# A routed-expert kernel: h of tiles 7 to 18 turned by DMA transposes of its words, and several small moves around it

## The chip, the cores and the metric

The kernel runs on one core of a Trainium2 chip. The core has TensorE (PE) with its weight loads (PEld), VectorE (DVE), ScalarE (ACT), GpSimd (POOL), SyncE (SP) and 16 DMA engines, each with its own list of instructions; semaphores order the lists against each other. The metric is the device time of one execution in microseconds, of which less is better.

## The reference

There are B=4 sequences of S=512 tokens with D=512 features. A layernormed x goes through a gated block whose weights are the context rows themselves; of four contexts each token takes the one that its id chooses. Then comes a mixture of six feed-forward experts, of which each sequence takes its top two:

```python
def _L0_xattn_ref(hidden_states, token_ids, Wg, Wu, Wd):      # Wg = Wu = Wd = ctx (4, 512, 512)
    expert_ids = jnp.minimum(tid // tokens_per_expert, E - 1)
    for e in range(E):
        g = jax.nn.silu(jnp.einsum('bsd,fd->bsf', hidden_states, Wg[e]))
        u = jnp.einsum('bsd,fd->bsf', hidden_states, Wu[e])
        y = jnp.einsum('bsf,df->bsd', g * u, Wd[e])
        out = jnp.where((expert_ids == e)[..., None], y, out)
...
    gate_probs = jax.nn.softmax(jnp.einsum('bd,ed->be', x.mean(axis=1), gate_W))
    topk_vals, topk_idx = jax.lax.top_k(gate_probs, TOP_K)    # renormalised to sum 1
    h = gelu(jnp.einsum('bsd,bkdf->bksf', x, W1[topk_idx]) + b1)      # F2 = 352
    eo = jnp.einsum('bksf,bkfd->bksd', h, W2[topk_idx]) + b2
    return jnp.einsum('bk,bksd->bsd', topk_vals, eo)
...
x = x + jnp.tanh(g_xattn[0]) * xattn(layernorm(x), ids, ctx)
x = x + jnp.tanh(g_ffn[0]) * ffn(layernorm(x))
```

Each product is made of split operands, a high part and a low part (hi·hi + lo·hi + hi·lo).

## The kernel before

**Stages.** After a setup that sorts the tokens by expert come TILES = 19 tiles of 128 sorted rows, one expert each (tile stage, some 30 to 145 us), and then four batches b = 0 to 3 of the second block.

**A tile.** GpSimd gathers the rows of tile j into one of RING places of x_ring (L502) and later writes the result back by a scatter (L511). VectorE takes the rows' mean and variance (rows_statistics, L661), GpSimd makes the inverse root (inverse_root, L506), VectorE normalises into h (L683). TensorE turns h by four transposes into bank 0 (transpose_h, L1192, its matmul at L1196); ScalarE copies the high part hT_hi (h_high, L965), VectorE makes the low part hT_lo (h_low, L689). The first product (12 matmuls, L1214) goes to bank 3, ScalarE takes silu of it (silu_of, L975), VectorE multiplies (up, L702) into a; TensorE turns a (transpose_a, L1199, L1205), a_high (L970) and a_low (L696) split it, and the second product (12 matmuls) gives y, which VectorE adds to x_ring (add, L668), with statistics for the second block (L673).

**The order of a step.** TensorE's step j is: turn a(j-1), turn h(j+1), first product of j, second product of j-1 (tile_step, L1313, and from PREP = 12 on the loop at L1422). ScalarE's is a_high(j-1), silu_of(j), h_high(j+1) (L1020). VectorE's is a_low, add, rows_statistics(j+2), statistics, up(j), normalise(j+2), h_low(j+1) (L754). GpSimd's is, tile by tile, inverse root, scatter, wait for an older scatter, gather (L555). All orders are written out by hand. In steps 12 to 18 work of batch 0 is put between: its rows are normalised and turned, ffn_h_high (L1024) splits them, the logits (L1349) and the gate (scale_logits, exponents, choose) follow.

**A batch.** hidden products with the first of two weight sets, gelu (L1065), output products, then the same with the second set. Weights come by SP's queue (load_experts, L403) and are split by ScalarE (split_high, L1056) and VectorE (split_low, L816). In batches 1 and 2 the normalised rows of the batch after are turned on the side: ScalarE parts the 32-bit words into their 16-bit halves (part_words, L1034), SP issues a DMA transpose of them (L454), and ScalarE joins the halves (join_words, L1043). ScalarE's list starts such a batch like this (L1105):

```python
if joined_ahead:
    split_high(b, 1, 2)
gelu_of(b, 0, 0, chosen)
```

where split_high(b, 1, 2) waits for w2 and the b2 rows of the second set, copies the b2 rows (L1062) and rounds w2 (L1063).

## Time and profile before

| | us |
|---|---|
| median of 3 runs (lowest, highest) | 281.7 (279.95, 281.95) |
| profiled execution | 281.29 |
| its span on the core | 279.5 |
| TensorE busy in the span | 272.1 (97%) |
| VectorE | 216.2 (77%) |
| ScalarE | 133.5 (48%) |
| GpSimd | 70.2 (25%) |

An engine's busy time counts its instructions alone, not its waits. Matmuls are pipelined: one that takes 0.39 us may start 0.23 after the one before. In rows of a timeline the first number is the start in us, the second the length, then engine, line, operation, what it writes and reads, and in brackets the idle time before it with what ended it. The chain of waits follows the last instruction back through what released it.

### The profile page before, as it was taken

The numbers are of one execution on the slowest core, as the hardware profiler recorded it, in microseconds if no ns is written. First come the engines' busy times: TensorE is split into PE (matmuls) and PEld (weight loads), VectorE is DVE, ScalarE is ACT, GpSimd is POOL, SyncE is SP. The second block draws the span as 40 slices with busy tenths as digits, with TensorE's granted clock in tenths as the row PEclk, the third lists the DMA queues.
The fourth block names the chain that finished last, engine by engine and source line by source line (L and its number), as shares of the span: only waits on it lengthen the run. The fifth ranks groups of instructions, "written<-read, shape, count | busy, mean of one in ns | idle before, by whom it ended". The sixth has DMA issues, their size and how long they took to land.

```text
span 279.5 us, 4519 instructions
## 1 busy us (share of the span) xinstructions
PE 272.1 (97%) x1400; PEld 222.3 (80%) x1400; DVE 216.2 (77%) x500; ACT 133.5 (48%) x216; POOL 70.2 (25%) x113
## 2 busy tenths in 40 slices
PE   8999999999999999999999999979999999999995
PEld 7878888888888888888778867858778777888783
DVE  8889888867777889687996669869698775958073
ACT  4844322223222233373628183889677995534020
POOL 5565265645444555324133000000000000000000
PEclk9999999999999999999999999999999999999999
DMA  6870042223255222319702717994199603940004
GB/s 214 290 254 0 5 119 105 79 75 111 82 135 199 82 75 78 75 45 300 205 38 87 240 53 233 228 276 151 31 306 211 189 0 113 315 160 2 0 0 150
DMA packets 32610, 37.10 MB, mean 133 GB/s; under 512 B 12584, under 2 KB 21038, under 8 KB 32588
## 3 DMA queue, kind: packets, MB, share of 16 engines
q1 hardware_dynamic: 29376, 26.69, 33.4%
q0 software_dynamic: 3040, 9.98, 11.4%
q8 instruction: 12, 0.20, 0.3%
q10 hardware_dynamic: 172, 0.15, 0.2%
q14 instruction: 10, 0.08, 0.1%
HBM read 25.52 MB, written 9.19 MB: 124 GB/s over the span
## 4 chain that ended last, share of the span: by engine, by line
PE 77%; SPq 6%; DMA 6%; ACT 5%; DVE 2%; issue 2%; DVEq 0%; ACTq 0%
PE bank L1214 38%; PE bank L1188 9%; PE bank L1189 8%; PE bank L1190 8%; DMA b_rows<-in_L_ffn_b 4%; PE bank L1205 3%; PE bank L1196 3%; PE bank L1266 3%; DMA raw_ctx<-in_ctx 2%; ACT w_hi L1063 2%; SPq L438 1%; DVE x_even L880 1%; SPq L435 1%; ACT act L1070 1%; SPq L433 1%
## 5 line engine op out<-in xcount | busy, mean ns | idle before, releaser
L1188 PE MATMUL bank<-w_lo,ctx_hi 128*128 128x512 f32 x80 | 31.7, 397 | 0.6 <-DVE ctx_lo L872 0.6
L1190 PE MATMUL bank<-w_hi,ctx_lo 128*128 128x512 f32 x80 | 31.2, 390 | 0.0
L1189 PE MATMUL bank<-w_hi,ctx_hi 128*128 128x512 f32 x80 | 31.2, 390 | 0.0
L978 ACT ACTIVATE a<-bank 128x512 f32<-128x512 f32 x19 | 11.4, 598 | 40.5 <-PE bank L1214 40.5
L973 ACT ACTIVATE aT_hi<-bank 128x512 fp32r<-128x512 f32 x18 | 10.8, 598 | 33.9 <-PE bank L1205 31.8
L1063 ACT ACTIVATE w_hi<-w_raw 128x512 fp32r<-128x512 f32 (+3 forms) x24 | 23.8, 1018 | 3.9 <-DMA w_raw<-in_L_ffn_W 3.9
L1188 PE MATMUL bank<-ctx_lo,w_hi 128*128 128x512 f32 x60 | 23.8, 397 | 1.2 <-ACT act L1070 1.2
L1214 PE MATMUL bank<-ctx_hi,hT_hi 128*128 (+1 forms) x80 | 23.3, 413 | 0.3 <-ACT hT_hi L968 0.3
L1189 PE MATMUL bank<-ctx_hi,w_hi 128*128 128x512 f32 x60 | 23.4, 391 | 0.0
L1190 PE MATMUL bank<-ctx_hi,w_lo 128*128 128x512 f32 x60 | 23.4, 390 | 0.0
L503 POOL DMA_INDIRECT x_ring<-in_x,get_rows x19 | 19.3, 1017 | 14.1 <-DVE put_rows L653 9.2
L871 DVE TENSOR_SCALAR ctx_hi<-act,mix 128x512 fp32r<-128x512 f32 x16 | 7.8, 486 | 19.3 <-ACT act L1070 19.2
L1070 ACT ACTIVATE act<-bank,tables 128x512 f32<-128x512 f32 x16 | 10.9, 684 | 22.9 <-PE bank L1190 22.8
L1214 PE MATMUL bank<-ctx_hi,hT_lo 128*128 (+1 forms) x80 | 21.6, 392 | 0.0
L1214 PE MATMUL bank<-ctx_lo,hT_hi 128*128 (+1 forms) x80 | 21.5, 391 | 0.0
L515 POOL DMA_INDIRECT x_scratch<-x_ring,put_rows x19 | 20.1, 1056 | 5.4 <-POOL x_ring L514 5.4
L698 DVE TENSOR_TENSOR aT_lo<-bank,aT_hi 128x512 fp32r<-128x512 f32 x18 | 12.4, 687 | 10.3 <-ACT aT_hi L973 10.3
L508 POOL TENSOR_TENSOR rstd<-ve,half 128x1 f32<-128x1 f32 x19 | 10.8, 570 | 36.2 <-DVE ve L666 36.2
L1214 PE MATMUL bank<-ctx_hi,aT_hi 128*128 (+1 forms) x72 | 19.9, 398 | 0.0
L1214 PE MATMUL bank<-ctx_hi,aT_lo 128*128 (+1 forms) x72 | 19.6, 392 | 0.0
L1214 PE MATMUL bank<-ctx_lo,aT_hi 128*128 (+1 forms) x72 | 19.3, 390 | 0.0
L1188 PEld LDWEIGHTS bank<-w_lo,ctx_hi 128*128 128x128 f32 x80 | 15.0, 188 | 4.6 <-issue 1.4
(221 smaller groups left out, 625.7 us busy)
## 6 DMA issues: line engine op xcount, KB each, us to landing
raw_ctx<-in_ctx SPq DMA_DIRECT2D x4, 1024.0 KB, 6.7
w_raw<-in_L_ffn_W SPq DMA_DIRECT2D x8, 512.0 KB, 4.8
x_even<-x_scratch SPq DMA_DIRECT2D x8, 257.0 KB, 3.9
w_raw<-in_L_ffn_W SPq DMA_DIRECT2D x8, 256.0 KB, 2.9
w_raw<-in_L_ffn_W SPq DMA_DIRECT2D x4, 448.0 KB
out<-x_even SPq DMA_DIRECT2D x7, 256.0 KB, 2.4
w_raw<-in_L_ffn_W SPq DMA_DIRECT2D x4, 384.0 KB, 7.2
x_odd<-x_scratch SPq DMA_DIRECT2D x4, 257.0 KB, 3.6
```

Source lines behind the costliest of these rows:

```text
L503: pool.indirect_dma_start(x_ring[:, r * DS:r * DS + D], None, x_rows, bass.IndirectOffsetOnAxis(get_rows[:, j:j + 1], 0)).then_inc(gathere ...
L508: pool.tensor_tensor(rstd1[:, :], ve1[:, :], half[:, 0:1], ALU.pow).then_inc(rstd_ready, 1)
L515: pool.indirect_dma_start(x1_rows, bass.IndirectOffsetOnAxis(put_rows[:, j:j + 1], 0), x_ring[:, r * DS:(r + 1) * DS], None).then_inc(scat ...
L698: dve.tensor_tensor(lo[:, :, :].rearrange("p k t -> p (k t)"), bank[:, :], hi[:, :, :].rearrange("p k t -> p (k t)").bitcast(FP32), ALU.su ...
L973: sc.activation(aT_hi[:, :, :].rearrange("p k t -> p (k t)"), aT_ps[:, :], ACT.Copy).then_inc(aT_hi_done, 1)
L978: sc.activation(a[:, :], z_bank(j)[:, :], ACT.Silu).then_inc(silu_done, 1)
L1063: sc.activation(part_of(w_hi[s], piece, s), part_of(w_raw[s], piece, s), ACT.Copy).then_inc(hi_done[s], 1)
L1070: sc.activation(act[:, c % 2, :], hid_ps[k % 2][:, :], ACT.Gelu, bias=b1_of(s, c, slice(0, P), chosen[s])).then_inc(gelu_done, 1)
L1188: pe.matmul(dst, s_hi, m_lo, start=first, stop=False)
L1189: pe.matmul(dst, s_hi, m_hi, start=False, stop=False)
L1190: return pe.matmul(dst, s_lo, m_hi, start=False, stop=last)
L1214: return pe.matmul(dst[:, :], src[:, k, :], weights[:, bass.ds(e * (KD * F1) + k * F1, F1)], start=first, stop=last)
```

## The change

1. **h of tiles 7 to 18** (TURNED = 7) is no longer turned by TensorE. VectorE normalises three tiles ahead instead of two (row_step). ScalarE parts h's words into halves (part_row), SP issues a DMA transpose for each tile (seven ahead of load_x1(0) in its list, five behind it), ScalarE joins the halves into hT_joined and copies that to hT_hi (join_row), ahead of silu_of, and VectorE's h_low reads hT_joined instead of the bank.
2. **GpSimd in the tile stage:** the ring has eight places (the eighth, x_eighth, in a region of act), the inverse root is made one tile further ahead and stands first in the loop, and one extra root stands behind the scatter of tile 3.
3. **The gate's exponents** go from ScalarE (Exp, with table loads) to GpSimd (a power of e); the logits of batch 0 and choose(0) stand one step later, and ffn_h_high(0) is spread over two steps. The splits of the first weights of batch 0 stand behind the tile loop.
4. **Batches 1 and 2:** the b2 rows are loaded ahead of the second weights; ScalarE's list starts with gelu; GpSimd rounds 128x1536 of w2 (round_w2) and joins the first quarter of the turned words (join_first).

Core of the diff ("..." marks what is left out):

```diff
-    RING = 7
+    RING = 8
+    TURNED = E + 3
...
+        def turned(j):
+            return TURNED <= j < TILES
         def hT_of(j):
-            return (hT1_hi, hT1_lo) if j == 1 else (hT_hi, hT_lo)
+            return (hT1_hi, hT1_lo) if j == 1 or (turned(j) and j % 2) else (hT_hi, hT_lo)
...
+                for e, rows in ((one, (64, 65, 96)), (two, (66, 67, 97))):
+                    for row in rows:
+                        sp.dma_start(b2_rows[row:row + 1, :], b2[bass.ds(e, 1), :]).then_inc(w2_here[1], 16)
                 sp.dma_start(part_of(second, 0), w1_cols(two, MB, MB + P)).then_inc(w1_here[1], 16)
...
+            turn_row_words(range(TURNED, EARLY + TURNED))
             sp.wait_ge(tiles_landed, EARLY)
             load_x1(0)
+            turn_row_words(range(EARLY + TURNED, TILES))
             sp.wait_ge(rows_done, 1)
             sp.wait_ge(pads_made, 2)
             load_experts(0)
...
             for j in range(1, TILES):
                 paired = j + 2 in PAIRED or j + 3 in PAIRED
-                if paired and j + AHEAD < TILES:
-                    inverse_root(j + AHEAD)
+                ahead_of = j + AHEAD + (j > TURNED - AHEAD)
+                if j == PREP + 2:
+                    exponents(0)
+                if paired and ahead_of < TILES:
+                    inverse_root(ahead_of)
                 scatter(j, j % RING)
...
+                if j == TURNED - AHEAD:
+                    inverse_root(ahead_of + 1)
                 landed(j - 1)
...
+            for b in range(0, B - 1):
+                if by_dma(b + 1):
+                    round_w2(b)
+                    join_first(b + 1)
+                exponents(b + 1)
...
+            def row_step(j, between=None):
+                add(j - 2, y_ps)
+                a_low(j - 1)
...
+                if j + 3 < TILES:
+                    rows_statistics(j + 3)
+                statistics(j - 2)
+                if j + 3 < TILES:
+                    normalise(j + 3)
+                up(j)
+                if j + 1 < TILES:
+                    h_low(j + 1)
...
+                    if j == TURNED - 2:
+                        rows_statistics(j + 3)
+                        normalise(j + 3)
...
+            def tile_step(j, between=None):
+                a_high(j - 1)
+                if turned(j + 1):
+                    join_row(j + 1)
+                if between:
+                    between()
+                silu_of(j)
+                if j + 1 < TURNED:
+                    h_high(j + 1)
+                if j == TURNED - 2:
+                    part_row(TURNED)
+                if j >= TURNED - 2 and turned(j + 3):
+                    part_row(j + 3)
...
-                if joined_ahead:
-                    split_high(b, 1, 2)
                 gelu_of(b, 0, 0, chosen)
                 split_high(b, 1, 0)
                 split_high(b, 1, 1)
                 gelu_of(b, 0, 1, chosen)
+                split_high(b, 1, 2)
                 if joined_ahead:
-                    join_words(b + 1, [0, 1])
-                else:
-                    split_high(b, 1, 2)
+                    join_words(b + 1, [1])
                 gelu_of(b, 0, 2, chosen)
...
                 transpose_a(j - 1)
-                if j in PAIRED:
+                if j in PAIRED and not turned(j + 1):
                     transpose_h(j + 1)
...
-                if j == PREP + 3:
+                if j == PREP + 4:
                     logits(0)
                 transpose_a(j - 1)
-                if j == PREP + 3:
-                    pe.wait_ge(neg_max_ready, 1)
-                if j + 1 < TILES:
-                    transpose_h(j + 1)
                 first_product(j, e)
```

How the rows of an engine's list move is shown at three places. In these rows a name's number tells one buffer from another, x2 means two alike, and brackets name the semaphores waited for.

TensorE's list at the start of step 6, before:

```order
L1209 ISA x2
L1205 MATMUL bank1<-ident,a 128x128 [waits aT_lo_done,a_ready]
L1205 MATMUL bank1<-ident,a 128x128 x3
L1196 MATMUL bank0<-ident,h 128x128 [waits hT_lo_done,h_ready]
L1196 MATMUL bank0<-ident,h 128x128 x3
L1214 ISA [waits a_ready,hT_hi_done]
L1214 MATMUL bank3<-ctx_hi_49,hT_hi 128x512
```

And of the changed kernel at the same place:

```order
L1307 ISA x2
L1303 MATMUL bank1<-ident,a 128x128 [waits aT_lo_done,a_ready]
L1303 MATMUL bank1<-ident,a 128x128 x3
L1312 ISA [waits a_ready,hT_hi_done]
L1312 MATMUL bank3<-ctx_hi_49,hT_hi 128x512
```

The four turns of h are gone, and the first product follows the turn of a.

ScalarE's list of steps 5 to 7, before (a<-bank3 is silu, hT_hi<-bank0 is h_high, aT_hi<-bank1 is a_high):

```order
L978 ACTIVATE a<-bank3 128x512 [waits z_done]
L968 ACTIVATE hT_hi<-bank0 128x512 [waits z_done,hT_done]
L973 ACTIVATE aT_hi<-bank1 128x512 [waits y_done,aT_done]
L978 ACTIVATE a<-bank3 128x512 [waits z_done]
L968 ACTIVATE hT_hi<-bank0 128x512 [waits z_done,hT_done]
```

And of the changed kernel:

```order
L1057 ACTIVATE a<-bank3 128x512 [waits z_done]
L1047 ACTIVATE hT_hi<-bank0 128x512 [waits z_done,hT_done]
L1103 ACTIVATE row_words_59<-h 128x1024 [waits h_ready] x2
L1052 ACTIVATE aT_hi<-bank1 128x512 [waits y_done,aT_done]
L1111 ACTIVATE hT_joined1_62<-row_words_T_60 128x2x512 [waits z_done,row_words_turned1]
L1113 ACTIVATE hT1_hi_57<-hT_joined1_62 128x512 [waits row_words_joined]
L1057 ACTIVATE a<-bank3 128x512 [waits z_done]
L1103 ACTIVATE row_words_59<-h 128x1024 [waits row_words_turned1,h_ready]
L1052 ACTIVATE aT_hi<-bank1 128x512 [waits y_done,aT_done]
```

Two partings (tiles 7 and 8) stand ahead of a_high(5), and the joining and copying of tile 7 ahead of silu of tile 6.

ScalarE's list at the start of batch 1, before (w_lo1<-b2_rows copies the b2 rows, act<-bank is gelu):

```order
L1062 ACTIVATE w_lo1<-b2_rows 64x512 [waits o_done,w2_here1]
L1063 ACTIVATE w_hi1<-w_raw1 128x1536
L1070 ISA [waits hid_done,a2_ready]
L1070 ACTIVATE act_53<-bank3,tables 128x512
L1063 ACTIVATE w_hi1<-w_raw1 128x512 [waits o_done,w1_here1]
```

And of the changed kernel:

```order
L1176 ISA [waits hid_done,a2_ready]
L1176 ACTIVATE act_53<-bank3,tables 128x512
L1169 ACTIVATE w_hi1<-w_raw1 128x512 [waits o_done,w1_here1]
L1169 ACTIVATE w_hi1<-w_raw1 128x4x192 [waits o_done,w1_rest_here1]
L1176 ISA [waits hid_done,a2_ready]
L1176 ACTIVATE act_53<-bank2,tables 128x512
L1165 ACTIVATE w_lo1<-b2_rows 64x512 [waits o_done,w2_here1]
```

The wait for w2_here1 stands behind two gelus now, and the rounding of 128x1536 has left the list.

## Rows read from the trace of the kernel before

**Rows 1.** The page's first part: busy us, share of the span, instructions.

```profile
PE 272.1 (97%) x1400; PEld 222.3 (80%) x1400; DVE 216.2 (77%) x500; ACT 133.5 (48%) x216; POOL 70.2 (25%) x113
```

**Rows 2.** Chain of waits in order of time, 99 to 130: start, us, what.

```profile
100.38 0.44 PE bank L1205 x4
100.82 0.44 PE bank L1196 x4
...
115.15 0.59 PE bank L1205 x4
...
128.50 0.63 PE bank L1196 x4
```

**Rows 3.** Busy us (instructions) by stretch, granted clock, DMA share, GB/s; step 6.

```profile
core 0: us, PE busy (x) PEld busy (x) DVE busy (x) ACT busy (x) POOL busy (x), PEclk, DMA share, GB/s
55.79:62.12 6.33, 6.33 (x33) 5.33 (x32) 4.88 (x11) 1.68 (x3) 3.04 (x5) 1.00 0.28 83
```

**Rows 4.** Instructions of words and words_T: duration ns min/median/max, first and last start.

```profile
L1040 ACT ACTIVATE words<-h x8: 1037/1041/1043, 175.6 to 212.3; 128x1024 uint16<-128x1024 uint16 x8
...
L454 SPq DMA_TRANSPOSE words_T<-words x8: 1292/1330/3289, 176.9 to 215.4; - x8
L1048 ACT ACTIVATE joined<-words_T x8: 1341/1355/1380, 186.9 to 224.6; 128x1024 uint16<-128x1024 uint16 x8
...
DMA to landing us min/median/max: 3.2/4.2/5.8
```

**Rows 5.** Timeline of VectorE, 82 to 89: the start of a tile's statistics and of the next.

```profile
83.72 0.68 DVE L664 BATCH_NORM_STATS2 stats<-x_ring 128x6 f32<-128x512 f32 x1
...
84.72 0.68 DVE L675 BATCH_NORM_STATS2 stats<-x_ring 128x6 f32<-128x512 f32 x1
```

**Rows 6.** Timeline of all engines, 54 to 60, around the start of step 6.

```profile
54.50 0.54 DVE L686 TENSOR_SCALAR h<-x_ring,mv,rstd 128x512 f32<-128x512 f32 x1
...
54.83 1.13 POOL L515 DMA_INDIRECT x_scratch<-x_ring,put_rows  x1 [0.29 <-POOL x_ring L514]
...
54.95 0.69 DVE L692 TENSOR_TENSOR hT_lo<-bank,hT_hi 128x512 fp32r<-128x512 f32 x1
...
56.42 0.60 ACT L973 ACTIVATE aT_hi<-bank 128x512 fp32r<-128x512 f32 x1 [2.08 <-PE bank L1205]
...
59.39 0.84 PE L1214 MATMUL bank<-ctx_hi,aT_hi 128*128 x3
...
59.59 0.60 ACT L978 ACTIVATE a<-bank 128x512 f32<-128x512 f32 x1 [2.58 <-PE bank L1214]
```

**Rows 7.** Timeline of TensorE, 182 to 189 and 220 to 222.

```profile
183.65 0.39 PE L1190 MATMUL bank<-ctx_hi,w_lo 128*128 128x512 f32 x1
185.25 0.50 PE L1188 MATMUL bank<-ctx_lo,w_hi 128*128 128x512 f32 x1 [1.20 <-ACT act L1070]
...
188.59 0.47 PE L1188 MATMUL bank<-w_lo,ctx_hi 128*128 128x512 f32 x1 [0.29 <-DVE ctx_lo L872]
...
221.25 0.47 PE L1188 MATMUL bank<-w_lo,ctx_hi 128*128 128x512 f32 x1 [0.32 <-DVE ctx_lo L872]
```

**Rows 8.** Timeline of all engines, 174 to 186.

```profile
174.79 2.03 SPq L438 DMA_DIRECT2D b_rows<-in_L_ffn_b  x6
...
182.49 0.63 ACT L1062 ACTIVATE w_lo<-b_rows 64x512 fp32r<-64x512 f32 x1 [1.56 <-DMA b_rows<-in_L_ffn_b]
...
184.53 0.67 ACT L1070 ACTIVATE act<-bank,tables 128x512 f32<-128x512 f32 x1
...
185.23 0.49 DVE L871 TENSOR_SCALAR ctx_hi<-act,mix 128x512 fp32r<-128x512 f32 x1 [1.97 <-ACT act L1070]
```

**Rows 9.** GpSimd's groups by shape: count | busy us, mean ns | idle before, releaser.

```profile
L508 POOL TENSOR_TENSOR rstd<-ve,half 128x1 f32<-128x1 f32 x19 | 10.8, 570 | 36.2 <-DVE ve L666 36.2
...
L500 POOL TENSOR_SCALAR w_raw<-col_h,pslot 128x128 f16<-128x128 f16 x3 | 2.0, 674 | 2.5 <-DVE pslot L631 2.5
...
L489 POOL MEMSET b_rows<- 128x512 f32 x1 | 0.5, 514 | 0.0
```

**Rows 10.** One line's instructions (L640, sorting): duration ns min/median/max, first and last start.

```profile
L640 DVE TENSOR_SCALAR w_raw<-col_h,pslot x13: 241/248/345, 6.1 to 8.1; 128x128 f16<-128x128 f16 x13
```

More of the change, by code:

```diff
@@ L221, in flamingo_kernel, with ring_place @@
         a2_lo = ctx_lo[:, 2 * KD * S:(2 * KD + FC) * S].rearrange("p (c t) -> p c t", t=S)
-        x_ring = sb("x_ring", [P, RING * DS])
+        x_ring = sb("x_ring", [P, (RING - 1) * DS])
+        x_eighth = at("x_eighth", [P, DS], FP32, place[1])
+        def ring_place(r, start, size):
+            return x_eighth[:, start:start + size] if r == RING - 1 else x_ring[:, r * DS + start:r * DS + start + size]
         used = [IDC * 2 * TILES // 2]
@@ L658, in ring_row @@
             def ring_row(j, start, size):
[L659 removed]
+                return ring_place(j % RING, start, size)
             def rows_statistics(j):
@@ L816, in split_low @@
             def split_low(b, s, piece):
-                place = (1, 2, 0)[piece] if s == 1 and by_dma(b + 1) else piece
-                dve.wait_ge(hi_done[s], len(PARTS) * b + place + 1)
+                dve.wait_ge(hi_done[s], len(PARTS) * b + piece + 1)
+                if s == 1 and piece == 2 and by_dma(b + 1):
+                    dve.wait_ge(w2_rounded, b)
                 raw, hi, lo = w_raw[s], w_hi[s], w_lo[s]
@@ L883, in _ @@
             for j in range(PREP, TILES):
-                if j == PREP + 3:
-                    scale_logits(0)
-                add(j - 2, y_ps)
-                a_low(j - 1)
-                if j + 2 < TILES:
-                    rows_statistics(j + 2)
-                statistics(j - 2)
-                up(j)
-                if j + 2 < TILES:
-                    normalise(j + 2)
-                if j + 1 < TILES:
-                    h_low(j + 1)
+                row_step(j, (lambda: scale_logits(0)) if j == PREP + 4 else None)
                 if j < PREP + 2:
```

137 lines of the change are left out of this document (89 added, 48 removed).

## The prediction

> **What bounds it now.** I read the page's first part, then the chain of waits in order of time, then the timeline stage by stage. TensorE is busy 272.1 of 279.5 us [rows 1], at a granted clock of 1.00 in the step whose window I show [rows 3] and in every other that I read. So a gain is work taken off PE, or a gap in PE's work that closes. In the chain a tile step is four turns of a(j-1), four turns of h(j+1), and the 24 matmuls of two products: the two groups of turns take 0.44 each, at 100.38 and 100.82 [rows 2]. In step 6 (55.79 to 62.12) VectorE works 4.88 of 6.33 us, ScalarE 1.68, GpSimd 3.04 [rows 3]. At two places a group of turns took longer, 0.59 at 115.15 and 0.63 at 128.50 [rows 2]: small waits, 0.34 in all. The other stretch to read is the turn from batch to batch, where PE does stand still [rows 7].
>
> **Term 1, the turns of h leave PE.** Tiles 7 to 18 are twelve, each with one group of four turns in a step: 12 x 0.435 = -5.2 us, and a step goes from about 6.35 to 5.92. This holds only if the new path (normalise, part into half words, DMA transpose, join, copy, low part) is ready for each step. The trace has its pieces already, since the batch stage turns its words in the same way: parting 1.04, the transpose 3.2/4.2/5.8 us from issue to landing, joining 1.36 [rows 4]; the copy to hT_hi is as large as that of aT_hi, 0.60 [rows 6].
>
> Steady state. VectorE keeps its eleven operations of a step, 4.88 us of 5.92 [rows 3]. ScalarE has 0.60 (a_high) + 1.36 + 0.60 (join, copy) + 0.60 (silu) + 1.04 (parting) = 4.2 of 5.92. From step 6, which begins at 55.79, a_high starts 0.63 later and silu 3.80 later [rows 6]; without the turn of h that is 3.4. In VectorE's new list add, a_low and two statistics stand ahead of normalise(j+3), which ends near S+4.3 (S: the step's start), and up(j) ends near S+5.0. Parting of tile j+3 runs from S+4.45 to S+5.5. Its joining stands behind a_high two steps later, at S + 11.84 + 1.23 = S+13.1. So a transpose may take 13.1 - 5.5 = 7.5 us with its handing over, and the longest of eight took 5.8 [rows 4]. PE sets the step, and this costs nothing: 1.7 us of cover over the longest, 3.3 over the median. If that cover is gone, up(j+1) is late by what goes beyond 7.5, at 0.5 to 1 us a step for each us of it, in eleven steps.
>
> **Term 2, the entry.** There the path isn't a step ahead yet, so I follow it through steps 5 to 7. h_low(6) ends at 55.64 [rows 6]. VectorE then takes the statistics of tile 8, 1.0 us from their first operation to the next one's start [rows 5]: 56.6. GpSimd's extra root stands behind the scatter that ends at 55.96 [rows 6], and takes 0.57 from 56.6 on [rows 9]: 57.2. normalise(8) takes 0.54 [rows 6]: 57.8. ScalarE parts it from 57.85 to 58.9, and only then comes a_high(5), which stands behind both partings now and started at 56.42 before [rows 6]: it ends at 59.4. PE reaches the second product of step 6, which began at 59.39 [rows 6], 0.435 earlier, at 58.96, and waits 0.45 for aT_hi.
>
> The words of tile 7 are parted behind its normalise (54.50 + 0.54, [rows 6]) from 55.1 to 56.2; their transpose lands at 59.4, 60.4 or 62.0 (3.2, 4.2, 5.8). Joining and copying (2.0) end at 62.4 by the median, silu(6) behind them at 63.0, up(6) (0.7) at 63.7. PE wants a(6) at 62.12 - 0.44 + 0.45 = 62.2: it waits 1.45. Bounds: 0.95 with the shortest landing (VectorE's list, which has normalise(9) ahead of up(6), holds it then), 3.0 with the longest. I take the median: 0.45 + 1.45 = **+1.9**, bounds +1.4 and +3.5. From step 8 on the lists are a step ahead.
>
> **Term 3, the rest of the tile stage.** The logits of batch 0 stand a step later and wait for the fourth piece of ffn_h_high, which is spread over two steps: +0.2, a third of one ScalarE copy of 0.6. The two small waits of the chain fall with the turns that had them: -0.34. Together **-0.1**. The exponents go from ScalarE to GpSimd's pow (as a root, 0.57, [rows 9]), and ScalarE's table loads go; in the chain neither holds PE: nothing.
>
> **Term 4, the batch turns.** At 183.65 PE starts a matmul, and the next only at 185.25, after a wait for gelu; the pitch is 0.23, so 1.37 is lost. ScalarE's list tells why: at 182.49 it copied rows of b2 after 1.56 us of waiting for their DMA, then rounded w2, and did the gelu at 184.53 [rows 8]. Two waits more, 0.29 at 188.59 and 0.32 at 221.25, are for low parts behind the same late copy [rows 7]; in the proportion of the first (1.37 lost for 1.20 shown) they cost 0.7 together. After the change gelu stands first, the rows of b2 are loaded ahead of the second weights, and GpSimd does the rounding: **-2.1**; from below nothing, if another wait takes the place (rival 1). What it moves: the six b2 issues take 2.03 us on SP's queue [rows 8], so the second weights go out that much later; ScalarE reads them behind its first gelu, and they have landed by then.
>
> GpSimd's price for this size the trace doesn't show. From below, a 128x512 memset in 0.51 is 1.0 ns an element, 1.5 us for 1536; from above, 128x128 in 0.67 is 5.3 ns, 8.1 us [rows 9]. The two joining copies of 512 are 0.5 to 2.7 each. I take 3 and 1 each, nearer the memset, which is nearer in size. From the b2 and w2 landing near 182.4 that ends at 187.5, or at 196 by the upper ends; the logits, which hang on the joined words, are wanted near 195 (the turn's PE work from 183.9 on). So the middle costs nothing, the upper end about 1 us in each of two turns.
>
> One page speaks against it. By the Trainium skill, "SBUF — State Buffer", section "SBUF: two separate sides", VectorE and GpSimd share a port pair as an exclusive lock for a whole instruction, so a VectorE operation with two SBUF inputs would stand until a GpSimd rounding that reads SBUF has ended. In this trace 13 VectorE operations took 0.241 to 0.345 us [rows 10] beside GpSimd's three of 0.67 [rows 9], and none was longer by one of these whole; no run here shows the lock with a wide GpSimd operation. What it would make of the time is rival 1.
>
> **Sum.** -5.2 + 1.9 - 0.1 - 2.1 = -5.5 from the profiled execution's 281.29 us (span 279.5 and 1.8 around it): 275.8. That execution is 0.4 below the median of the runs, 281.7, so against the median it is -2.1%.
>
> **Rivals.**
> 1. GpSimd takes ScalarE's place at the turns. At the middle of its two bounds the rounding is 4.8 us, 182.4 to 187.2. The next weighing on VectorE stood at 185.23 [rows 8] and is due at 184.6 when gelu follows PE; waiting for GpSimd's whole operation it loses 2.6, in two turns 5.2: 275.8 + 5.2 = **281.0**. For it: the two work side by side on wide tiles for the first time, and VectorE's low part of w2 waits for the rounding too. Against: [rows 10]. Half of it gives 278.4. Chance 0.12.
> 2. The lists make a step longer than PE does: up(j) stands behind normalise(j+3) in VectorE's list, and that behind a root and a parting. At 0.3 us in each of eleven steps it is 275.8 + 3.3 = **279.1**. For it: roots waited 36.2 us in all for VectorE's statistics [rows 9], so each is made in the last moment, and now stands between two operations of the same list. Against: 1.0 us of each step is free on VectorE, and a root is 0.57. Chance 0.13.
> 3. The other side: transposes land late, as SP's queue has loads of x1 between them and an issue took up to 3.3 us [rows 4]. From 7.5 us of latency steps lengthen; at 9.0 in every step it is 1.5 x 0.5 x 11 = +8.3, **284.1**, and from about 9.1 slower by over 1%. Against: the longest of eight was 5.8. Chance 0.07.
> 4. No change: the entry costs its upper bound (+1.6 more), the turns give nothing back (+2.1), and the steps are 0.2 longer (+2.2): **281.7**. Chance 0.06.
>
> **Numbers.** The forecast has 0.62, with a range of its own from 274 (entry at its lower bound, turns a little better) to 277.5 (entry at its upper bound). Within 1% of 281.7, about what a measurement of this kernel can tell from no change, is 278.9 to 284.5. Faster: the forecast, the milder half of 1 and of 2: 0.73. Slower: rival 3 and a trace of 1: 0.08. The rest: 0.19. The range 273.8 to 280.0 takes in rival 2 and half of 1, and leaves out 3, 4 and the full 1.
>
> **What would show it.** Right: no turn of h on PE after tile 6 and steps of 5.92; waits of PE of about 0.45 and 1.45 in steps 6 and 7 and nowhere else in the stage; joining waits for a DMA at tile 7 alone; the gap of 185.25 gone, since gelu no longer stands behind a DMA. Wrong: steps over 6.1, and what up waits for (root, parting or a landing) tells rival 2 from 3; a VectorE operation of several us beside GpSimd's rounding, or ScalarE and PE waiting for GpSimd's joining copies, is rival 1.

## The result, and the profile after

The changed kernel takes 277.67 us (median of 4, 277.57 to 278.45), the kernel before on the same occasion 281.61: a ratio of 0.987 with a 95% interval of 0.984 to 0.990, so 1.3% faster. On a second occasion it was 278.15 beside 281.57 (0.986, 0.983 to 0.990). The forecast was 275.8: right in its direction, in its range and in most of its places, and 1.9 us too good.

The page's first part of the changed kernel, to be read beside [rows 1]:

```profile
PE 267.1 (97%) x1352; PEld 217.6 (79%) x1352; DVE 220.6 (80%) x508; ACT 145.0 (52%) x213; POOL 91.5 (33%) x124
```

TensorE has 48 instructions less (twelve tiles of four turns) and 5.0 us less to do; ScalarE has 11.5 more and GpSimd 21.3 more. The span fell by 2.9 (279.5 to 276.6; the traced execution took 278.45).

Where the time went is seen by the same marks of TensorE's work in both traces:

| stretch of TensorE's work | before | after | difference | prediction |
|---|---|---|---|---|
| start to step 2 | 30.01 | 30.48 | +0.47 | 0 |
| step 2 to the turn of a(18) (from 140.67; from 137.93) | 110.66 | 107.45 | -3.21 | -3.4 |
| from there to the last matmul (275.77; 272.97) | 135.10 | 135.04 | -0.06 | -2.1 |

The first row is the first load of context, 5.30 us in one chain of waits and 5.77 in the other. In ten other traces, with an edit or without, it was 5.3 to 6.5; it differs from execution to execution. The tile stage came out as worked. Nearly the whole miss is in the batches.

**The tile stage.** Busy us by stretch (as [rows 3]) of step 6, the entry, and step 10 of the changed kernel:

```profile
core 0: us, PE busy (x) PEld busy (x) DVE busy (x) ACT busy (x) POOL busy (x), PEclk, DMA share, GB/s
56.44:64.08 7.64, 6.38 (x30) 4.70 (x28) 5.79 (x15) 4.88 (x7) 3.12 (x5) 1.00 0.63 139
81.90:87.83 5.93, 5.93 (x29) 4.90 (x28) 5.02 (x11) 4.15 (x5) 3.81 (x5) 1.00 0.59 133
```

Step 10 takes 5.93 and TensorE is busy in all of it; the step of [rows 3] took 6.33. ScalarE's 4.15 is the 4.2 of the prediction. The chain of waits shows nothing but TensorE in steps 8 to 13 (one turn of a, 24 matmuls, as in [rows 2] without the second turn; in step 15 it goes round by VectorE and ScalarE to the logits, which lose 0.25):

```profile
82.06 0.44 PE bank L1303 x4
82.50 5.49 PE bank L1312 x24
```

The transposes of h (one tile's instructions, as [rows 4]):

```profile
L467 SPq DMA_TRANSPOSE row_words_T<-row_words x12: 1232/1233/1342, 56.9 to 118.9; - x12
L1111 ACT ACTIVATE hT_joined<-row_words_T x12: 1357/1363/1372, 60.1 to 126.9; 128x1024 uint16<-128x1024 uint16 x12
...
DMA to landing us min/median/max: 3.1/4.5/5.7
```

The batch stage's 3.2/4.2/5.8 was a true price for them, and no joining had to wait for one.

**The entry**, on the timeline (as [rows 6]):

```profile
57.39 0.57 POOL L539 TENSOR_TENSOR rstd<-ve,half 128x1 f32<-128x1 f32 x1 [0.77 <-DVE ve L729]
...
58.63 1.06 ACT L1103 ACTIVATE row_words<-h 128x1024 uint16<-128x1024 uint16 x1 [1.85 <-DVE h L750]
...
59.60 0.58 ACT L1052 ACTIVATE aT_hi<-bank 128x512 fp32r<-128x512 f32 x1
...
60.21 0.69 DVE L763 TENSOR_TENSOR aT_lo<-bank,aT_hi 128x512 fp32r<-128x512 f32 x1 [0.95 <-ACT aT_hi L1052]
60.32 1.19 PE L1312 MATMUL bank<-ctx_hi,aT_hi 128*128 x4 [0.51 <-ACT aT_hi L1052]
...
64.08 0.65 PE L1303 MATMUL bank<-ident,a 128*128 128x128 f32 x4 [0.75 <-DVE a L769]
```

GpSimd's root of tile 8, then its parting on ScalarE, then a_high(5), then TensorE: 0.51 of waiting. Step 6 took 7.64 where 5.92 would do, so 1.72 was lost, and step 5 was 0.19 longer than before: 1.9 in all, the number of term 2. (Step 5 is 6.43 to 6.77 in the other traces and 6.69 here; before it was 6.50. Its 0.19 is scatter.) Its two parts were cut otherwise: from start to start they are 0.67 and 0.90 for 0.45 and 1.45. The words of tile 7 landed early (joining began at 60.08, straight behind a_high), and the second wait is VectorE's list behind the late a_high, for which it had waited 0.95 at 60.21.

**The batches.** A turn is here the passage from one batch to the next. What follows are TensorE's losses of more than 0.3 us in the batches. At 183.65 to 188.59 of [rows 7] both gaps are gone. In their place the timeline of TensorE has two new ones:

```profile
170.76 0.39 PE L1288 MATMUL bank<-w_hi,ctx_lo 128*128 128x512 f32 x1
172.21 0.47 PE L1509 MATMUL bank<-w_hi,ctx_hi 128*128 128x512 f32 x1 [1.07 <-DVE ctx_hi L950]
...
216.77 0.39 PE L1288 MATMUL bank<-ctx_hi,w_lo 128*128 128x512 f32 x1
218.43 0.47 PE L1286 MATMUL bank<-w_lo,ctx_hi 128*128 128x512 f32 x1 [1.27 <-DVE ctx_lo L963]
```

From start to start, less the pitch of 0.23, they are 1.22 us in batch 0, where nothing was lost before, and 1.43 in batch 2, where 0.49 was (221.25 of [rows 7]). Both wait for VectorE's weighing, which multiplies gelu's result by its expert's share and splits the product into a high and a low part. The experiments ask what made VectorE late.

The first has its cause in the chain of waits. From the logits on it goes through the gate's arithmetic:

```profile
161.64 0.16 DVE logit L876
...
162.31 1.37 POOL expo L590
...
163.71 0.16 DVE esum L882
...
171.32 0.76 DVE ctx_hi L950
...
172.21 0.47 PE bank L1509
```

GpSimd's power of six elements takes 1.37, not the 0.57 that a root of 128x1 had in [rows 9]. From the first of these operations to the reciprocal at 163.89 it is 2.25 us; in the trace of before the same way, with ScalarE's exponents, was 1.04 (164.33 to 165.37). Behind it VectorE's list has no wait of more than 0.23 up to the weighing, so the delay arrives whole: from the first of these operations to the matmul of 172.21 it is 10.57, and 9.52 to the same matmul before (164.33 to 173.85).

The second shows on the timeline of batch 2 (VectorE's L962 and L963 are the two halves of a weighing; away from GpSimd they take 0.49 and 0.75):

```profile
213.62 1.47 POOL L614 CAST w_hi<-w_raw 128x1536 fp32r<-128x1536 f32 x1 [17.92 <-DMA w_raw<-in_L_ffn_W]
213.82 1.55 DVE L962 TENSOR_SCALAR ctx_hi<-act,mix 128x512 fp32r<-128x512 f32 x1
...
215.03 2.08 POOL L622 COPY joined<-words_T 128x512 uint16<-128x512 uint16 x2
215.40 1.08 DVE L963 SCALAR_TENSOR_TENSOR ctx_lo<-act,mix,ctx_hi 128x512 fp32r<-128x512 f32 x1
216.40 0.98 DVE L962 TENSOR_SCALAR ctx_hi<-act,mix 128x512 fp32r<-128x512 f32 x1
```

GpSimd's rounding is as cheap as the lower bound said (1.47 for 1.5 to 8.1), and VectorE's weighing that begins beside it ends 0.28 us behind its end. In batch 1 too a weighing began beside the rounding (0.81 long from 180.92, also ending 0.28 behind), but there TensorE lost nothing.

### The profile page after: what moved, and what is told of

Its sections match the earlier page's. It is cut to its first block, busy times and chain, and to the rows that moved or that the text cites. A ratio compares the mean times of both kernels' runs of the same rounds, so it can differ in the third digit from the quotient of the medians.

```text
span 276.6 us, 4459 instructions
## 1 busy us (share of the span) xinstructions
PE 267.1 (97%) x1352; PEld 217.6 (79%) x1352; DVE 220.6 (80%) x508; ACT 145.0 (52%) x213; POOL 91.5 (33%) x124
## 4 chain that ended last, share of the span: by engine, by line
PE 75%; DVE 10%; DMA 4%; issue 4%; ACT 4%; POOL 2%; SPq 1%; DVEq 0%; ACTq 0%; POOLq 0%
PE bank L1312 32%; PE bank L1286 10%; PE bank L1288 10%; PE bank L1287 10%; PE bank L1303 3%; PE bank L1364 3%; DMA w_raw<-in_L_ffn_W 2%; DMA raw_ctx<-in_ctx 2%; PE bank L1509 1%; DVE ctx_hi L962 1%; PE bank L1510 1%; POOL expo L590 1%; DVE x_odd L971 1%; DVE x_even L971 1%; PE bank L1294 1%
## 5 line engine op out<-in xcount | busy, mean ns | idle before, releaser
L546 POOL DMA_INDIRECT x_scratch<-x_ring,put_rows x17 | 22.4, 1318 | 4.9 <-POOL x_ring L545 4.4
L1169 ACT ACTIVATE w_hi<-w_raw 128x512 fp32r<-128x512 f32 (+3 forms) x22 | 20.9, 975 | 5.9 <-DMA w_raw<-in_L_ffn_W 5.9
L534 POOL DMA_INDIRECT x_ring<-in_x,get_rows x17 | 17.5, 1030 | 13.9 <-DVE put_rows L716 9.6
L910 DVE TENSOR_TENSOR w_lo<-w_raw,w_hi 128x512 fp32r<-128x512 f32 (+2 forms) x16 | 17.0, 1088 | 3.4 <-ACT w_hi L1169 3.3
L545 POOL TENSOR_TENSOR x_ring<-x_ring,half 128x1 f32<-128x1 f32 x17 | 13.4, 787 | 14.4 <-DVE x_ring L740 14.4
```

What stands on the lines that cost most here:

```text
L534: pool.indirect_dma_start(ring_place(r, 0, D), None, x_rows, bass.IndirectOffsetOnAxis(get_rows[:, j:j + 1], 0)).then_inc(gathered[r], 16)
L545: chain.run(pool.tensor_tensor(deviation, deviation, half[:, 0:1], ALU.pow), apart=True)
L546: pool.indirect_dma_start(x1_rows, bass.IndirectOffsetOnAxis(put_rows[:, j:j + 1], 0), ring_place(r, 0, DS), None).then_inc(scattered[r], 16)
L910: dve.tensor_tensor(part_of(lo, piece), part_of(raw, piece), part_of(hi, piece).bitcast(FP32), ALU.subtract).then_inc(lo_done[s], 1)
L1169: sc.activation(part_of(w_hi[s], piece, s), part_of(w_raw[s], piece, s), ACT.Copy).then_inc(hi_done[s], 1)
```

## The experiments

All are made from the changed kernel. On each occasion its variants ran beside the kernel before, whose median moved between 280.4 and 281.7 from one occasion to another; differences under about half a per cent between kernels of two occasions are therefore taken from the traces, not from the times.

### Exponents back on ScalarE

```diff
-                exponents(b + 1)
...
                     ffn_h_high(b + 1, t_ps)
+                    bring_tables(ACT.Exp)
+                    sc.wait_ge(neg_max_ready, b + 2)
+                    sc.activation(expo[:, :], logit[:, :], ACT.Exp, bias=neg_max[:, 0:1],
+                                  accum_out=esum[:, 0:1]).then_inc(expo_done, 1)
+                    bring_tables(ACT.Gelu)
```

> The changed kernel with the exponents of batches 1 to 3 back on ScalarE (Exp, its table loads and the sum beside it), all else as changed. In the changed kernel's trace TensorE loses 1.22 us at 172.21, waiting for VectorE's weighing, and from the logits to the reciprocal VectorE takes 2.25 us (161.64 to 163.89, with 1.36 of it GpSimd's power of six elements) where it took 1.04 before (164.33 to 165.37). Theory A, the exponents on GpSimd make that wait: the 2.25 goes back to about 1.05, the wait falls to under 0.2 us, and the time by about 1.1, from 277.7 to 276.6. Theory B, VectorE's list as a whole is late there because TensorE now comes 2.7 us earlier, whoever does the exponents: the wait stays at 0.9 or more and the time within 0.3 of 277.7.

Measured: 276.09 (276.01 to 276.78), 0.980 of the kernel before (0.976 to 0.985). The gate's arithmetic on VectorE's timeline:

```profile
162.60 0.15 DVE L875 TENSOR_SCALAR logit<-bank 1x6 f32<-1x6 f32 x1 [0.20 <-PE bank L1466]
162.79 0.15 DVE L877 TENSOR_REDUCE neg_max<-logit 1x1 f32<-1x6 f32 x1
163.63 0.15 DVE L886 RECIPROCAL einv<-esum 1x1 f32<-1x1 f32 x1 [0.70 <-ACT expo L1233]
```

It is 1.03 again, and TensorE's wait of 1.22 in batch 0 is gone; from 161 on no gap in its trace is over 0.2. The edit takes more back than the power: the subtraction of the maximum and the sum leave VectorE's list with it. So theory A holds: the exponents, moved to GpSimd to spare ScalarE two table loads, lengthened VectorE's list at the one place where TensorE waits for it. The table loads (1.28 each) stand in a pause of ScalarE there and cost TensorE nothing. The gap of batch 2 is gone as well: there the second weights landed sooner against the weighing (rounding 210.49 to 211.96, weighing from 212.39 on).

### VectorE's low part of w2 into the pause

```diff
                     scale_logits(b + 1)
+                    if not joined_ahead:
+                        split_low(b, 1, 2)
                     choose(b + 1)
                     mixing(b + 1)
-                if not joined_ahead:
+                if not joined_ahead and not more:
                     split_low(b, 1, 2)
```

> The changed kernel with one VectorE operation of batch 0 moved: the low part of w2 (128x1024, 1.21 us at 165.60) goes from behind the gate's arithmetic to between the logits and it, where VectorE waits 1.49 us for GpSimd's exponents. Theory A, VectorE's chain from the logits to the weighing makes the 1.22 us wait, and that operation can lie in the pause: the wait falls to under 0.2 us, the time to 276.5. Theory B, something else releases TensorE there (gelu, a weight): the wait stays over 0.9 and the time within 0.3 of 277.7.

Measured: 278.38 (277.86 to 278.67; 0.989, 0.984 to 0.993), and 1.15 us still lost at 171.97. By the numbers theory B; by the timeline it is neither:

```profile
162.10 1.21 DVE L919 TENSOR_TENSOR w_lo<-w_raw,w_hi 128x1024 fp32r<-128x1024 f32 x1
...
162.27 2.27 POOL L590 TENSOR_TENSOR expo<-euler,logit 1x6 f32<-1x6 f32 x1 [14.69 <-DVE logit L878]
```

The pause was filled and came back: GpSimd's power, 1.31 to 1.37 in all other cases, took 2.27 and ended at 164.54, 1.23 behind the end of VectorE's operation (163.31). GpSimd stood until VectorE was done, though the two share no data. By the Trainium skill, "SBUF — State Buffer", section "SBUF: two separate sides", a VectorE operation with two SBUF inputs that starts first holds the shared port pair for the whole instruction, and a GpSimd operation that reads SBUF fully blocks; this trace agrees. In the same run batch 1 lost 0.95, with the weighing 1.39 long beside the rounding.

### Rounding back on ScalarE

```diff
-                    round_w2(b)
...
-                    copied = sc.activation(w_lo[1][LW:P, WN - D:WN], b2_rows[LW:P, :], ACT.Copy)
-                    if by_dma(b + 1):
-                        copied.then_inc(hi_done[1], 1)
-                        return
+                    sc.activation(w_lo[1][LW:P, WN - D:WN], b2_rows[LW:P, :], ACT.Copy)
```

> The changed kernel with the rounding of 128x1536 of w2 in batches 1 and 2 on ScalarE, behind its copy of the b2 rows; GpSimd keeps only the joining. In the changed kernel's batch 2 the first weighing takes 1.55 us at 213.82 beside GpSimd's rounding (213.62 to 215.09) where it takes 0.49 elsewhere, the next 1.08 for 0.75 and the one after 0.98 for 0.49 beside the joining, and TensorE loses 1.43 at 218.43. Theory C, GpSimd's wide operation holds VectorE's: that first weighing takes about 0.5, the loss of 1.43 falls to 0.5 or less, and the time falls by 0.9 to 1.4, unless ScalarE's own 1.49 makes its third gelu late, which would show as a wait of TensorE or VectorE for gelu of up to 1.5 us in both batches. Theory D, VectorE is late from what stands ahead of it (low part behind a weight load, residuals): the weighings take 0.5 but start as late, the loss stays over 1.0 and the time within 0.3 of 277.7.

Measured: 277.45 (277.05 to 278.19; 0.986, 0.981 to 0.991). The weighing of batch 2:

```profile
212.79 0.48 DVE L957 TENSOR_SCALAR ctx_hi<-act,mix 128x512 fp32r<-128x512 f32 x1
213.30 0.75 DVE L958 SCALAR_TENSOR_TENSOR ctx_lo<-act,mix,ctx_hi 128x512 fp32r<-128x512 f32 x1
```

0.48 and 0.75, and no loss at that place: theory C. By time it gains 0.2 us on the median of the changed kernel, less than expected and not clear of noise. ScalarE's 1.49 delays its third gelu a little (VectorE waited 0.41 and 0.30 for it), and the 1.43 of the first trace isn't lost in every execution. The changed kernel's second trace, run again without an edit, shows that:

> The changed kernel itself once more, unaltered, for a second trace and for its time beside the kernel before on another occasion. If TensorE's 1.22 us wait in batch 0 comes from the order of the work (exponents on GpSimd), it is there again, at 1.1 to 1.3. If the loss at the turns hangs on when the second weights land against VectorE's weighing, it differs from the 0 and 1.43 us of the first trace in at least one of the batches 1 and 2, and in each turn a weighing that begins during the rounding ends 0.28 us behind it. The time is 277 to 278.5.

It lost 1.23 at 173.40 again (the order's doing), nothing at batch 1's turn, and 0.47 in batch 2, where the rounding (213.21 to 214.68) ended just as the weighing was due and only the joining hit it.

### Rounding twice

```diff
+                chain.run(pool.tensor_copy(part_of(w_hi[1], 2, 1), part_of(w_raw[1], 2, 1)))
                 pool.tensor_copy(part_of(w_hi[1], 2, 1), part_of(w_raw[1], 2, 1)).then_inc(w2_rounded, 1)
```

> The changed kernel with GpSimd rounding its 128x1536 of w2 twice, one behind the other, in batches 1 and 2; the result is the same. Theory C, a GpSimd operation on wide SBUF tiles holds VectorE's weighing until its end: in all traces so far a weighing that begins beside the rounding ends 0.28 us behind it, and one to 1.5 us more of it makes another weighing wait; TensorE then loses 1 to 2.5 us in each of the two batches, for 278.5 to 280.5 in all. Rival: the weighings are only slowed a little while GpSimd runs (shared bandwidth), so a longer run of GpSimd adds 0.3 to 0.5 us to one more of them and the time stays within 0.5 of 277.7.

Measured: 279.11 (278.86 to 280.92; 0.996, 0.993 to 0.999), with 0.59 lost in batch 1 and 1.07 in batch 2. The timeline of batch 1:

```profile
179.95 1.47 POOL L614 CAST w_hi<-w_raw 128x1536 fp32r<-128x1536 f32 x1 [16.01 <-DMA w_raw<-in_L_ffn_W]
181.19 0.51 DVE L963 TENSOR_SCALAR ctx_hi<-act,mix 128x512 fp32r<-128x512 f32 x1
181.49 1.54 POOL L615 CAST w_hi<-w_raw 128x1536 fp32r<-128x1536 f32 x1
181.74 1.84 DVE L964 SCALAR_TENSOR_TENSOR ctx_lo<-act,mix,ctx_hi 128x512 fp32r<-128x512 f32 x1
```

The second rounding caught the second half of the weighing, 1.84 for 0.75, ended 183.58 against the rounding's 183.03. So VectorE's operation waits until GpSimd's is over; a share of bandwidth would have cost a part. It is not quite a wait of its whole length: it ends 0.28 (first half) or 0.55 (second) behind GpSimd's, 0.2 less than it takes alone, and why is open. So this work of the two engines excludes each other, and what it costs TensorE hangs on when the second weights land: 0, 0.47, 0.95 and 1.43 were seen with one rounding in the turns where the two met.

### The turns' lists as they were

```diff
+                if joined_ahead:
+                    split_high(b, 1, 2)
                 gelu_of(b, 0, 0, chosen)
                 split_high(b, 1, 0)
                 split_high(b, 1, 1)
                 gelu_of(b, 0, 1, chosen)
-                split_high(b, 1, 2)
                 if joined_ahead:
-                    join_words(b + 1, [1])
+                    join_words(b + 1, [0, 1])
+                else:
+                    split_high(b, 1, 2)
```

with the b2 rows behind the second weights, and neither rounding nor joining on GpSimd.

> The changed kernel with the lists of batches 1 and 2 as they were (b2 rows behind the second weights, ScalarE copying them and rounding w2 ahead of the first gelu, joining all four quarters; nothing of it on GpSimd), with the turned h and the exponents as changed. If the turns' three gaps of the kernel before were made by that list (prediction, term 4), they come back: 1.37, 0.45 and 0.49 us, and the 1.43 of batch 2 goes, so the time is 277.7 + 2.3 - 1.4 = 278.6. If the turns gain nothing in either form, because TensorE's earlier arrival is eaten by loads that come no sooner, it stays within 0.3 of 277.7.

Measured: 280.33 (median of 10, 279.43 to 281.65; 0.996, 0.993 to 0.998), 1.7 more than expected. TensorE's waits of batches 1 and 2, in the longest of the ten executions (281.65):

```profile
184.32 0.50 PE L1277 MATMUL bank<-ctx_lo,w_hi 128*128 128x512 f32 x1 [1.06 <-ACT act L1165]
...
187.66 0.47 PE L1277 MATMUL bank<-w_lo,ctx_hi 128*128 128x512 f32 x1 [0.28 <-DVE ctx_lo L955]
...
218.25 0.50 PE L1277 MATMUL bank<-ctx_lo,w_hi 128*128 128x512 f32 x1 [1.12 <-ACT act L1165]
...
221.59 0.47 PE L1277 MATMUL bank<-w_lo,ctx_hi 128*128 128x512 f32 x1 [0.33 <-DVE ctx_lo L955]
```

The gaps of [rows 7] come back, and batch 2 now has the large one too, likely because TensorE arrives sooner and the loads don't. So the new lists of the turns are worth 2.7 us by the medians (280.33 to 277.67) and 2.4 by the ratios, even with GpSimd in VectorE's way: the mechanism of term 4 is right. In this trace the wait of batch 0 (1.25 at 173.03, GpSimd's exponents) is there as well.

### The turned h nearly alone

This is the run of the old lists with the exponents of batches 1 to 3 on ScalarE too; both diffs stand above.

> The turned h nearly alone: the changed kernel with the exponents of batches 1 to 3 on ScalarE and the lists of batches 1 and 2 as they were before. By the prediction's terms 1 to 3 the tile stage alone gives -3.4, and its trace has given -3.2: 281.7 - 3.2 = 278.5, with TensorE's gaps of 1.2 to 1.4, 0.45 and 0.5 us in batches 1 and 2 as before and none of 1.2 in batch 0. Rival: the gain of the tile stage is eaten later by waits for loads that come no sooner, and the time is 280.3 or more, as with the old turns and GpSimd's exponents (280.33).

Measured: 279.53 (median of 10, 277.45 to 280.92; 0.994, 0.991 to 0.997), between the two expectations. Its trace, an execution of 277.84, has steps of 5.92 and no wait behind the gate of batch 0, and loses 0.41, 0.48 and 0.46 at the turns; the executions with the median's time were not traced. That a late copy of b2 rows costs 0.4 in one execution and 1.3 in another, as the two traces with the old lists show, would make such a spread, but it isn't shown for these. Beside the run with the exponents on ScalarE (276.09) it says once more what the new lists are worth: 3.4 by the medians.

### The entry's order

```diff
                 a_high(j - 1)
+                if j == TURNED - 1:
+                    part_row(TURNED + 1)
                 if turned(j + 1):
                     join_row(j + 1)
...
-                if j >= TURNED - 2 and turned(j + 3):
+                if j >= TURNED - 1 and turned(j + 3):
                     part_row(j + 3)
```

> The changed kernel with one ScalarE instruction moved: the parting of tile 8 goes from ahead of a_high(5) to behind it. In the changed kernel a_high(5) starts at 59.60, behind the parting of 58.63, TensorE waits 0.51 for it at 60.32 and 0.75 more at 64.08 for up(6), and step 6 takes 7.64 us where 5.92 would do. Theory (prediction, term 2): a_high(5) goes back to about 57.1, the first wait is gone, a_low(5) and the statistics behind it come about 1.0 sooner, up(6) ends at about 63.2 rather than 64.0, and step 6 takes 6.8: time -0.8, to 276.9. Rival: what holds step 6 is the root of tile 8 and the landing of tile 7's words, which stay where they are; then the wait moves whole to the second place, step 6 stays at 7.4 or more and the time within 0.3 of 277.7.

Measured: 277.06 (276.89 to 277.45; 0.987, 0.984 to 0.989 on its own occasion, so the gain can't be read from the times). From the timeline:

```profile
57.13 0.60 ACT L1052 ACTIVATE aT_hi<-bank 128x512 fp32r<-128x512 f32 x1 [0.23 <-PE bank L1305]
...
63.43 0.66 PE L1305 MATMUL bank<-ident,a 128*128 128x128 f32 x4 [0.82 <-DVE a L769]
```

and from its chain of waits:

```profile
56.98 3.13 DMA row_words_T<-row_words
...
60.13 1.38 ACT hT_joined L1111
...
62.07 0.59 ACT a L1057
...
62.69 0.70 DVE a L769
```

a_high(5) is at 57.13, its wait is gone, and step 6 takes 6.94 (56.49 to 63.43), 0.70 less; 0.8 was expected. That the parting of tile 8 stood ahead of a_high(5) was the cause of that part of the entry. The second wait stays, 0.82, and has changed its owner: the chain now goes through the landing of tile 7's words, their joining and silu(6), for which up(6) waited 0.20. That is the wait that term 2 had named, and the rest of the entry can't be had from the order of a_high.

### Two and three transposes for one

```diff
                     sp.wait_ge(row_words_made, j - TURNED + 1)
+                    for _ in range(1):
+                        sp.dma_start_transpose(spare_T[:, j % 2], row_words[:, j % 2].rearrange("p g d -> p (g d)")).then_inc(
+                            row_words_turned[j % 2], 16)
                     sp.dma_start_transpose(row_words_T[:, j % 2], row_words[:, j % 2].rearrange("p g d -> p (g d)")).then_inc(
                         row_words_turned[j % 2], 16)
```

with ScalarE's waits doubled (two) or tripled (three).

> The changed kernel with a second DMA transpose ahead of each of the twelve of h's words, of the same words into a spare place, and ScalarE waiting for both; the result is the same. An issue takes SP 1.23 us and the landings were 3.1/4.5/5.7, so joining can begin 1.3 to 3 us later in each step. Theory (prediction, term 1): from the issue on there are some 7.5 us of cover, so the steps stay at 5.92 and only the entry grows, by 1.2 to 2: 278.9 to 279.7. Rival: the cover is much smaller than reckoned, and steps of 8 to 18 grow to 6.2 or more, over 281.

> As the run with two transposes, but with two spare ones ahead of each of the twelve, and SP holding a tile's three until the three of the tile before have landed. Theory (prediction, term 1): landing of the last comes at 7 to 10 us from the first issue, about at the end of the cover of 7.5 or beyond it; steps grow by 0.5 to 1 us for each us over, to 6.0 to 8.0, with joining waiting for the DMA in most steps: 281 to 290. Rival: ScalarE's list has more slack than reckoned and the steps stay at 5.92 with 280 or less.

Measured: 284.55 with two (2 runs, 283.63 and 285.47; 1.013, 1.008 to 1.018) and 300.85 with three (2 runs; 1.071, 1.066 to 1.076). Both times are above what was expected, the first by about 5, the second by about 11. With two, ScalarE's joining on the timeline, the first, the fifth and the eighth:

```profile
64.53 1.34 ACT L1115 ACTIVATE hT_joined<-row_words_T 128x1024 uint16<-128x1024 uint16 x1 [4.37 <-DMA row_words_T<-row_words]
...
89.39 1.38 ACT L1115 ACTIVATE hT_joined<-row_words_T 128x1024 uint16<-128x1024 uint16 x1 [0.91 <-DMA row_words_T<-row_words]
...
108.09 1.37 ACT L1115 ACTIVATE hT_joined<-row_words_T 128x1024 uint16<-128x1024 uint16 x1 [1.84 <-DMA row_words_T<-row_words]
```

and steps 7 and 8:

```profile
67.80:75.41 7.61, 7.61 (x29) 6.23 (x29) 5.57 (x12) 4.19 (x6) 3.01 (x4) 0.78 0.46 106
75.41:81.32 5.91, 5.91 (x29) 4.90 (x28) 5.02 (x11) 4.15 (x5) 2.54 (x4) 1.00 0.99 162
```

The steady steps stayed at 5.92 with joining waiting up to 1.03 for the DMA. In step 10 the words were there 8.4 us from the first issue (81.01 to 89.39) and it cost nothing: the cover is there, and the 7.5 reckoned was on the strict side. One step grew, to 6.37, behind the 1.84; the issues for that tile stood behind load_x1 on SP's queue until 99.98. The entry was what went wrong. The words of tile 7 were ready to join 7.7 us from the first issue (56.86 to 64.53), so step 6 took 11.37 instead of 7.64, where 1.2 to 2 more had been expected. From 62.20 to 67.80, while joining waited, the DMA share was 0.99 (0.63 in the entry with one transpose). And as TensorE had stood still for 4.47, step 7 ran at a mean granted clock of 0.78 and took 7.61. Before the turn of batch 1's rows it lost 2.44 more, waiting for VectorE's normalise. With three, step 6 took 13.31, joining waits for the DMA in all twelve steps, 35.4 us in all, and steps 8 to 11 grow from 6.17 to 9.42. So a third transpose is beyond the cover in every step, and a second one within it in nearly all.

### Both repairs together

> The changed kernel with both repairs that gave something: exponents of batches 1 to 3 on ScalarE, and the parting of tile 8 behind a_high(5). If the two are independent, -1.6 and -0.6 add up: 277.67 - 2.2 = 275.5. If the earlier end of the tile stage is only waited away in batch 0 or at the weight loads, it is that of the exponents alone, 276.1.

> As the run with the two repairs, and with the rounding of w2 in batches 1 and 2 on ScalarE too, so that GpSimd has only the joining there. If GpSimd's rounding still hits VectorE's weighing in some executions (by when the second weights land), this is faster by 0.2 to 0.8: 274.7 to 275.3. If with the exponents on ScalarE the rounding comes early enough in all of them, ScalarE's extra 1.49 buys nothing: 275.5, within 0.3 of the run with two repairs.

Measured: 275.59 (274.62 to 275.85; 0.982, 0.979 to 0.984) for the exponents on ScalarE with the entry's order, and 275.58 (275.47 to 276.2; 0.983, 0.980 to 0.985) with the rounding on ScalarE too. On one occasion, side by side, they are the same. In the trace with GpSimd's rounding it is over at 210.26 in batch 2, before the next weighing, and meets only the end of one in batch 1 (0.57 for 0.48); TensorE loses nothing at either turn. That this comes from a gate decided sooner, and weights asked for sooner, is likely and not shown. Against the exponents alone (276.09, 0.980 on another occasion) the entry's gain is 0.5 by the medians and nothing by the ratios; in the traces step 6 is 6.89 for 7.63. Either version is the fastest of all kernels here.

## Why the prediction was right, and where it was off

- **Term 1, -5.2 for twelve turns**: right. Steps of 5.92 to 5.93, TensorE never short of a turned tile in the steady state, ScalarE at 4.15 of 4.2, normalise ending 4.48 into a step (4.3) and up 5.07 (5.0). The transposes cost what the trace of the batch stage had said, and the runs with two and three show the cover.
- **Term 2, +1.9 for the entry**: right in sum (1.72 and 0.19), in part by luck. By the pitch the first wait cost 0.67 for 0.45, and the second 0.90 for 1.45: the words landed in about the shortest time, not the median, for which the term itself has +1.4, and VectorE's list behind the late a_high held up(6). With a_high in its place the landing held it, as the term says. No joining waited for a DMA in the changed kernel, where one at tile 7 had been named as a sign.
- **Term 3, -0.1**: the step that failed. The sentence that the exponents go to GpSimd "as a root, 0.57" and hold TensorE nowhere took a price of one element per partition for six in one, and looked for TensorE's wait in the tile stage alone. It is 1.37, with one VectorE operation more on each side; the way from the logits to the reciprocal grew by 1.21, and in batch 0 TensorE waits for what stands behind it in VectorE's list. In the trace of before TensorE lost nothing there; that TensorE arrives 2.7 us sooner is not the cause: with ScalarE's exponents the logits come at 162.60 and nothing is lost, and in the second trace of the changed kernel they come at 162.81, later, and 1.23 is lost. It cost 1.2 in both traces of the changed kernel. The rest of the term (the logits' 0.2 to 0.3, against small waits of before) was about right.
- **Term 4, -2.1**: right in what it closes. The two gaps of batch 1 are gone, and the old lists put back cost 2.7 us; the third, in batch 2, was to close and became 1.43. Its price for the rounding was too high (3 for 1.47) and its conclusion, "the middle costs nothing", too low: GpSimd's time isn't what counts but when it falls.
- **Rival 1** was the mechanism of the rest, with VectorE's weighing waiting for the end of GpSimd's rounding as it said, at 1.1 us longer (1.55 for 0.49) and not 2.6; it came in both turns and cost TensorE something in one. By the Trainium skill, "SBUF — State Buffer", section "SBUF: two separate sides", that is the lock of the shared port pair: an operation with two SBUF inputs, as the weighing's second half, contends with a GpSimd operation that reads SBUF, and a tensor_scalar, as its first half, can. The measurement sides with the page. The row held against it, [rows 10], was a true one, but for another operation. On the timeline of the kernel before, thirteen fp16 operations on 128x128 ran beside three of GpSimd's all the while, and none waited:

```profile
6.06 2.32 DVE L640 TENSOR_SCALAR w_raw<-col_h,pslot 128x128 f16<-128x128 f16 x13
6.08 1.99 POOL L500 TENSOR_SCALAR w_raw<-col_h,pslot 128x128 f16<-128x128 f16 x3 [2.45 <-DVE pslot L631]
```

  So not every VectorE operation waits, and the mistake was to carry the row over to fp32 tiles of 128x512. Which difference decides wasn't tried.
- **Rival 2** and **rival 3** did not come: steps of 5.92, no joining late. Rival 4 is out.
- **The sum.** The profiled execution took 278.45, 2.65 over the forecast: 0.47 for the first load, 0.19 in the tile stage, and 2.04 in the batches (1.22 for the exponents, 0.94 by which the third gap grew, 0.28 for its closing, as 2.1 was forecast and the two gaps that closed gave 1.82, less 0.4 of small differences that were not followed up). By the medians the miss is 1.9. With the exponents back and the entry in order the kernel takes 275.6.

## What to carry to other kernels

Work moved to an idle engine must be priced at its own shape and placed in the list that waits for it: the six-element power was 2.4 times the one-element root, and it stood in the one chain that TensorE ends up waiting for. GpSimd beside VectorE isn't a free engine: before giving it wide tiles, look at which VectorE operations are due in that stretch, and expect those that read SBUF alone, on wide fp32 tiles, to wait until GpSimd's operation is over, or the reverse. A pipelined path with DMA in it is judged in two places, in its steady state by its cover and at its entry by following each list by hand; both worked here, and a repair of one instruction's place at the entry was worth 0.7 us in the trace.

## What the runs showed of the hardware that was not expected

- GpSimd's power on 1x6 takes 1.31 to 1.37 us, its root on 128x1 0.57: more by 0.75 for six elements in a row on one partition than for one element on each of 128.
- A GpSimd operation of a few elements also waits for a wide VectorE one (2.27 for 1.34 beside a 128x1024 subtraction of 1.21), and the first half of VectorE's weighing ended about 0.28 us behind GpSimd's rounding in each turn where it began beside it.
- VectorE's adds that read a bank and one SBUF tile did not wait. Four of them beside the rounding, in batch 2 of the changed kernel's second trace, took 2.49, and four at the end of the trace, where GpSimd is idle, 2.46:

```profile
212.18 2.49 DVE L971 TENSOR_TENSOR x_odd<-bank,x_odd 128x512 f32<-128x512 f32 x4
213.21 1.47 POOL L614 CAST w_hi<-w_raw 128x1536 fp32r<-128x1536 f32 x1 [16.37 <-DMA w_raw<-in_L_ffn_W]
```

- In the tile stage of the changed kernel GpSimd's root of the second statistics takes 0.82 (median) where it took 0.55, and the scatter 1.42 for 1.05. The roots begin now while VectorE normalises; that it is the same wait is likely by the starts and ends, but was not tried. The last root of the stage, beside VectorE's 128x1536 subtraction of 1.75, takes 2.01. Neither is on the path.
- After a wait of TensorE of 4.47 us (two transposes for one) the granted clock was 0.51 for the next 2.2 us, nearly all at the lower of its levels (1.2 GHz), and 0.69 for two more, and the step of 5.92 took 7.61. The waits of 0.5 to 1.4 us in the changed kernel left it at 1.00 or next to it.
- In most traces of variants, and in the second one of the changed kernel itself (0.69), TensorE also lost 0.4 to 0.8 us at 156 to 157, ahead of the transposes of batch 1's rows, for VectorE's normalise. The two traces laid side by side above don't have it, and its cause wasn't tried.
